# Twelve raw places and a ring of six for a streamed adjacency matrix, in place of eight and eight

## The reference

```
def block(x, layer): return x + layer(maximum(layernorm(x), 0), adj)

L0(h) = (adj / rowsum) @ h @ W_in + (adj.T / colsum) @ h @ W_out
L1(h) = n = silu((adj @ h) @ W1 + b1);  silu((adj @ n) @ W1 + b1)
L2(h) = relu(((adj_norm @ h) @ W2) + b2)
L3(h) = relu((adj_norm @ (h @ W3)) + b3)
adj_norm = (adj + I) * d_inv_sqrt[:, None] * d_inv_sqrt[None, :],  d = rowsum(adj + I)
x: (4096, 128) f32, adj: (4096, 4096) f32
```

## Time and profile before

| | us |
|---|---|
| median of 3 runs | 1154.41 (1153.81 to 1154.59) |
| the profiled execution | 1153.61 |
| its span, first to last instruction | 1151.8 |

### The profile page before, as it was taken

How to read it: one execution, slowest core, us unless ns; L and a number is a source line. 1 busy time by engine, 2 the same in 40 slices (tenths; PEclk the granted TensorE clock), 3 DMA queues, 4 the chain that set the end, 5 groups by cost and what they waited for, 6 DMA issues and landing times.

```text
span 1151.8 us, 14790 instructions
## 1 busy us (share of the span) xinstructions
PE 1120.3 (97%) x5120; PEld 919.1 (80%) x5120; DVE 1046.6 (91%) x1419; ACT 909.1 (79%) x1265; POOL 48.0 (4%) x40
## 2 busy tenths in 40 slices
PE   4999999999999899999999999999999999999997
PEld 3778888888876678888888887888888888888886
DVE  5999989989899999987988999999999999998985
ACT  6888897887777868787887787888777788776772
POOL 0000000000000000000000211201112111000000
PEclk9999999999999999999999999999999999999999
DMA  9999999999988889999999999999999999998984
GB/s 348 339 337 394 391 410 377 352 407 381 341 301 304 300 282 400 401 381 362 396 346 381 312 383 332 369 379 340 376 340 358 379 327 376 353 394 331 401 330 171
DMA packets 113546, 408.36 MB, mean 355 GB/s; under 512 B 12608, under 2 KB 13632, under 8 KB 113472
## 3 DMA queue, kind: packets, MB, share of 16 engines
q1 hardware_dynamic: 113472, 407.42, 95.1%
HBM read 405.27 MB, written 2.10 MB: 354 GB/s over the span
## 4 chain that ended last, share of the span: by engine, by line
PE 83%; DVE 10%; ACT 4%; issue 2%; DMA 0%; ACTq 0%; DVEq 0%
PE bank L604 52%; PE bank L608 27%; DVE a_lo L385 6%; PE bank L615 3%; ACT a_hi L270 3%; PE bank L636 1%; ACT act_raw L294 1%; DVE x_sb L482 1%; DVE h_lo L408 1%; DVE zt L390 1%; DVE stats L415 0%; ACT a_hi L268 0%; DMA x_sb<-in_x_dram 0%; DVE zt L394 0%; DVE mv L419 0%
## 5 line engine op out<-in xcount | busy, mean ns | idle before, releaser
L385 DVE TENSOR_TENSOR a_lo<-raw,a_hi 128x1024 fp32r<-128x1024 f32 x768 | 898.3, 1219 | 64.7 <-ACT a_hi L268 49.9
L268 ACT ACTIVATE a_hi<-raw 128x1024 fp32r<-128x1024 f32 x512 | 520.6, 1054 | 81.1 <-DMA raw<-in_adj_t_dram 65.5
L604 PE MATMUL bank<-a_hi,h_hi 128*128 128x512 f32 x1536 | 480.0, 394 | 14.6 <-ACT a_hi L270 14.5
L608 PE MATMUL bank<-a_lo,h_hi 128*128 128x512 f32 x1536 | 479.1, 393 | 9.3 <-DVE a_lo L385 7.7
L604 PE MATMUL bank<-a_hi,h_lo 128*128 128x512 f32 x1536 | 474.6, 390 | 0.0
L608 PEld LDWEIGHTS bank<-a_lo,h_hi 128*128 128x128 f32 x1536 | 285.0, 188 | 85.8 <-DVE a_lo L385 28.6
L604 PEld LDWEIGHTS bank<-a_hi,h_hi 128*128 128x128 f32 x1536 | 284.2, 188 | 72.7 <-DVE h_lo L408 14.5
L604 PEld LDWEIGHTS bank<-a_hi,h_lo 128*128 128x128 f32 x1536 | 288.9, 188 | 61.4
L270 ACT ACTIVATE a_hi<-raw 128x1024 fp32r<-128x1024 f32 x256 | 269.7, 1055 | 29.4 <-DMA raw<-in_adj_dram 8.5
L303 ACT ACTIVATE act_raw<-x_sb,lnbias,lnscale 128x128 f32<-128x128 f32 x96 | 39.7, 484 | 47.0 <-DVE lnbias L443 47.0
L252 POOL TENSOR_TENSOR std<-mv,eps_sb 128x4 f32<-128x4 f32 x16 | 17.4, 1088 | 931.6 <-DVE mv L419 931.6
(11 more groups left out here) (50 smaller groups left out, 183.4 us busy)
## 6 DMA issues: line engine op xcount, KB each, us to landing
raw<-in_adj_t_dram SPq DMA_DIRECT2D x640, 512.0 KB, 6.5
raw<-in_adj_dram SPq DMA_DIRECT2D x128, 512.0 KB, 6.3
x_sb<-in_x_dram SPq DMA_DIRECT2D x4, 512.0 KB, 10.5
out_dram<-x_sb SPq DMA_DIRECT2D x8, 256.0 KB, 7.0
w_sb<-in_L_gnn_W_dram SPq DMA_DIRECT2D x3, 64.0 KB, 11.3
b_sb<-in_L_gnn_b_dram SPq DMA_DIRECT2D x3, 64.0 KB, 8.1
w_sb<-in_L_gnn_W_in_dram SPq DMA_DIRECT2D x1, 64.0 KB, 12.3
w_sb<-in_L_gnn_W_out_dram SPq DMA_DIRECT2D x1, 64.0 KB, 12.3
```

The lines of the kernel that those rows point to most:

```text
L268: act.activation(sub(a_hi, n), sub_raw(n), ACT.Copy).then_inc(sub_hi, 1)
L385: dve.tensor_tensor(sub(a_lo, n), sub_raw(n), sub(a_hi, n).bitcast(F32), ALU.subtract).then_inc(sub_lo, 1)
L604: pe.matmul(bank[half][:, :], weights, hi_a[:, half * GW:(half + 1) * GW], start=start and weights is hi_w, stop=False)
L608: last = pe.matmul(bank[half][:, :], hi_w, lo_a[:, half * GW:(half + 1) * GW], start=False, stop=stop)
```

## The change

The counts of places are changed: `RAWS` from 8 to 12, `RING` from 8 to 6. A raw place takes 4 KB of each partition, a ring place twice that (one of `a_hi`, one of `a_lo`), so that the memory stays as it is: 8 x 4 + 8 x 8 = 96 KB before, 12 x 4 + 6 x 8 = 96 KB after.

```
-    RING = 8
-    RAWS = 8
+    RING = 6
+    RAWS = 12
```

## The result

The changed kernel takes 1151.26 us (median of 16 runs, 1151.07 to 1151.47), against 1153.51 us of the kernel before in the runs beside them (1152.61 to 1155.41): a ratio of 0.9979, 95% interval 0.9971 to 0.9987. The forecast was 2.28 us less than before, the measured difference of the medians is 2.25 us; by the interval it lies between 1.5 and 3.3 us. The absolute 1152.1 of the forecast is 0.9 us too high, since it was laid on the median of three runs (1154.41), and with thirteen more runs of the same kernel that median is 1153.51.

A forecast was written before the change was run, and what follows sets the result against it. TensorE, busy 97%, bounds the kernel, losing 3.27 us in five groups, mostly behind late loads at their heads. Gains of 0.95, 0.74, 0.27 and 0.32 sum to 2.28 us: 1154.41 - 2.28 = 1152.1 us, range 1151.0 to 1154.6.

The forecast's parts named there:

- The loss per group and its cause: At group heads a late load delays ScalarE's prod_t copy (L317), and VectorE hands the lateness on to TensorE.
- B to E: Four successive groups of 32 substeps, timed between L615 marks, that ran 1.31, 1.03, 0.27 and 0.32 us too long.
- The size: TensorE gets back the smaller of copy delay and group loss: 0.95, 0.74, 0.27 and 0.32 us, sum 2.28 us.
- A: Group of 32 substeps in sweep 2, 0.34 us too long; forecast to stay so, its copy already waiting for TensorE.
- VectorE follows by a hair: In C, five a_lo steps of 1.13 us bring substep 5 to 721.9; the shift asks for 721.94.
- The spare rate of the queue: DMA queue can move 410 GB/s against a mean 361: 2.3 MB or 4.4 tiles spare per group, filling four new places.
- The start of the program costs nothing: Four more loads delay x blocks 2 and 3 and weights by 5.1 us; first reader at least 23 us off: nil.
- The ring costs nothing: With two ring places fewer, ScalarE's lead held to six tiles is lead thrown away or covered anyway: cost nil.
- the cover of 0.55 us: After substep 13's held a_hi ScalarE is free at 640.34; the layernorm activation, waiting for lnbias, starts at 640.89.
- rival (c): Ring holds substep 13's a_hi past lnbias: 0.81 us in each of five tight groups, 1156.1 us; chance 0.08.
- Rival (a): Loads are spent as they land, the queue's rate rather than the number of places holding the head: 1154.4 us; chance 0.17.
- Rival (b): Earlier head also takes the remaining 0.99 us of the first three tight groups: 3.27 in all, 1151.1 us; chance 0.17.

## Why the prediction was right, step by step

- **The loss per group and its cause.** The late copies of B to E were read as the cause of their losses. Putting the late loads back at one head alone gave that group 0.70 us of loss and no other one any. This is shown. The way from there to TensorE was read too simply: the prediction has VectorE go "from instruction to instruction", but in C of the kernel before it idles twice on that way for an a_hi behind the layernorm activation, 0.46 us at 737.22 and 1.06 us at 750.62. The lateness is handed on all the same, since these waits hang on lnbias, which VectorE itself makes: C's copy is late by 0.74 us, and lnbias by 0.74.
- **The size.** The smaller of the copy's delay and the group's loss gave 0.95, 0.74, 0.27 and 0.32 us; measured were 1.01, 0.74, 0.27 and 0.32. In all 2.28 forecast, 2.34 in these four groups, 0.04 in A, and 2.25 between the medians. In D and E the forecast simply took the whole loss, so that only B and C test the rule. B's 0.06 too little is a load behind the copy: z_out of B was 0.94 us late, its L514 1.03. In the run with the ring alone the same rule would have missed C by more than half. It came out here because loads behind the copies added little in this one execution. And an agreement to 0.03 us between the medians is luck, with a kernel before whose runs lie 2.8 us apart and an interval of 1.5 to 3.3 us.
- **VectorE follows by a hair.** It did: C came out at the forecast 45.62.
- **The spare rate of the queue.** Ten places sufficed as twelve did, so that two tiles ahead, not 4.4, were needed. That the queue has something to spare was right; how much it must have, no run here tells. In B's stretch the queue now moves 367 GB/s instead of 361, and over 210 us on end 381. The Trainium skill's limit of about 358 GB/s in "DMA: Bandwidth & Descriptors", section Specifications, doesn't bind here, with one core at work: the trace disagrees with it, before and after.
- **The start of the program costs nothing.** With four loads more ahead of x blocks 2 and 3, TensorE reaches the first group mark of sweep 1 at 447.80 us, against 447.83. The weight loads wait for a_lo 9.8 us in 14 to 110 us and 15.7 in 320 to 426, against 8.9 and 15.6.
- **The ring costs nothing.** 1.0002 alone, with the cover of 0.55 us that was read in A; the changed kernel shows 0.53 (640.85 - 639.36 - 0.96). At five places the cover is gone, and the loss is 0.81 us a group, the figure that rival (c) used. That rival was wrong in its place: it needed one place fewer. A ring of eight was not run with enough raw places; six and seven, with ten raw places each, lie 0.03 us apart.
- **Rival (a), nothing gained,** fell with the result. **Rival (b), the rest too,** fell as well: A to C keep their 0.3 us, and VectorE's idle time behind the activation holds no load. That this idle time makes the 0.3 us was right: with the activation one substep later it is all but gone, and so are they.
- **The base.** The absolute time was forecast 0.9 us too high. The three runs of before lay in the upper half of a spread from 1151.5 to 1155.4 us over all sets.

## What to carry to other kernels

Two sets of buffers in a row hold different things: the one ahead of an engine hides how late its input may be, the one behind it how far it may run ahead, and a place is worth something only where that very wait is the last one. Read each count by its own wait (here: one copy at the head of a group that came late behind a load; one activation that had 0.5 us of cover), and move memory from the one whose wait nobody is behind. Once such a count is enough, more of it is worth nothing, as ten and twelve raw places or six and seven ring places show. One ring place too few cost 2.3 us here, one raw place too few 0.3 us in the median and up to 1.6 in single runs.

## What the runs showed beyond that

Enough raw places make the time steady as well as shorter. With eight places the runs of a kernel lie 1.7 to 3.3 us apart (1152.96 to 1154.68 with the ring of six, 1152.15 to 1155.44 for the kernel before in the last set of runs), with nine 1.6 us, with ten or twelve 0.25 to 0.5 us (1151.11 to 1151.36; 1151.07 to 1151.47; 1151.09 to 1151.61). The likely reason is that small differences in when a load lands reach the time of the kernel while loads are on the path. Of that the traces show only a part: in the two profiled executions with eight raw places B lost 1.01 and 1.68 us over the changed kernel, C 0.74 and 0.66, D 0.27 and nothing, E 0.32 and nothing. These are two kernels (ring of eight and of six); that runs of the same kernel differ in this way was not profiled, and what makes single loads land earlier or later was not tried.
